# Decoder layer on one core: the scan's state and retrieval as 32 x 32 blocks, and the second quantile's edge counts on TensorE

## The reference

```
def step(S, inp):                       # per batch element and head, S is 16 x 16
    q_t, k_t, v_t, beta_t = inp
    retrieval = einsum('bhij,bhj->bhi', S, k_t)
    S = S + einsum('bhi,bhj->bhij', beta_t * (v_t - retrieval), k_t)
    o_t = einsum('bhij,bhj->bhi', S, q_t)
    return (S, o_t)
...
_, out_t = lax.scan(step, S0, (q, k, v, beta))          # 512 steps, 16 heads
...
attn = softmax(where(mask == 0, NEG, x @ ctx.T / 16)); x = attn @ ctx
...
s = 127 / quantile(abs(x), 0.995); q = clip(round(x * s), -128, 127) / s
out = quant(gelu(quant(h) @ ternary(w1).T)) @ ternary(w2).T
```

## Time and profile before

| | |
|---|---|
| median of 3 runs | 969.68 us |
| the profiled execution, its own time | 975.51 us |
| its span, first to last instruction | 973.6 us |
| mean granted TensorE clock, share of full | 0.95 |
| scan, first to last state matmul | 45.3 to 602.8 us |
| second quantile, first sample to scale | 888.8 to 923.5 us |

### The profile page before, as it was taken

How to read it: one execution, slowest core, us unless ns; L and a number is a source line. 1 busy time by engine, 2 the same in 40 slices (tenths; PEclk the granted TensorE clock), 3 DMA queues, 4 the chain that set the end, 5 groups by cost and what they waited for, 6 DMA issues and landing times.

```text
span 973.6 us, 19722 instructions
## 1 busy us (share of the span) xinstructions
PE 861.1 (88%) x6257; PEld 657.5 (68%) x6257; DVE 822.7 (85%) x2508; ACT 699.3 (72%) x1819; POOL 523.5 (54%) x501
## 2 busy tenths in 40 slices
PE   7899999999999999999999999879999813995285
PEld 6687887787787787787787777556666513443264
DVE  4789999989999999999999988756777787899797
ACT  4688888887788788788778766536777750895095
POOL 5446656665465565565455544445888860980100
PEclk9899999999999999999999999989999965998599
DMA  9900000000000000004000000133110000000023
GB/s 162 159 1 13 7 7 13 6 7 12 7 8 11 8 7 11 8 7 140 8 8 10 9 6 8 36 132 130 66 66 0 2 1 0 1 1 1 0 68 106
DMA packets 28573, 30.50 MB, mean 31 GB/s; under 512 B 5548, under 2 KB 23864, under 8 KB 28472
## 3 DMA queue, kind: packets, MB, share of 16 engines
q1 hardware_dynamic: 28256, 29.12, 11.9%
q10 hardware_dynamic: 216, 0.14, 0.1%
HBM read 20.85 MB, written 4.19 MB: 26 GB/s over the span
## 4 chain that ended last, share of the span: by engine, by line
PE 65%; ACT 15%; DVE 12%; issue 6%; POOL 1%; DMA 1%; ACTq 0%; POOLq 0%; DVEq 0%
PE ps L2002 10%; PE ps L1933 5%; PE psY L1971 5%; PE psX L1971 4%; PE ps L2118 4%; PE psG L1956 4%; PE ps L1994 4%; ACT arena L733 3%; PE psG L1950 3%; PE ps L2060 3%; PE psX L2139 3%; PE psY L2139 2%; PE ps L2325 2%; PE psG L1951 2%; ACT arena L698 2%
## 5 line engine op out<-in xcount | busy, mean ns | idle before, releaser
L523 POOL TENSOR_SCALAR_AFFINE_SELECT arena<-arena 128x2048 f32<-128x2048 f32 x32 | 64.5, 2015 | 163.3 <-DVE arena L1308 163.3
L538 POOL TENSOR_TENSOR work<-work,half 128x16 f32<-128x16 f32 x32 | 94.9, 2966 | 2.7
L527 POOL TENSOR_SCALAR_AFFINE_SELECT arena<-arena 128x2048 f32<-128x2048 f32 x32 | 92.1, 2879 | 2.2
L698 ACT ACTIVATE arena<-ps,nparity 32x128 f32<-32x128 f32 x248 | 76.2, 353 | 18.8 <-PE ps L1933 17.3
L1994 PE MATMUL ps<-work 32*128 32x256 f32 x512 | 82.6, 402 | 3.0 <-ACT arena L733 2.9
L733 ACT ACTIVATE arena<-ps 128x512 f32<-128x512 f32 x128 | 69.3, 593 | 16.6 <-PE ps L1994 15.8
L1994 PEld LDWEIGHTS ps<-work 32*128 32x128 f32 x512 | 53.5, 184 | 37.3 <-issue 28.3
L1327 DVE TENSOR_REDUCE arena<-arena 128x64 f32<-128x256 f32 (+1 forms) x96 | 65.9, 687 | 3.3
L1971 PE MATMUL psY<-work,arena 128*128 128x96 f32 (+1 forms) x512 | 61.7, 280 | 3.1 <-ACT arena L698 2.0
L1971 PEld LDWEIGHTS psY<-work,arena 128*128 128x128 f32 x512 | 60.0, 196 | 6.5 <-issue 6.5
L537 POOL TENSOR_SCALAR work<-work 128x16 f32<-128x16 f32 x32 | 8.1, 254 | 102.1 <-ACT work L750 102.1
(11 more groups left out here) (362 smaller groups left out, 2498.1 us busy)
## 6 DMA issues: line engine op xcount, KB each, us to landing
arena<-in_mask_BxSxS_ik SPq DMA_DIRECT2D x8, 1024.0 KB, 6.7
xs<-arena SPq DMA_DIRECT2D x256, 16.0 KB, 1.8
arena<-in_ctx SPq DMA_DIRECT2D x8, 512.0 KB, 4.2
out<-xs SPq DMA_DIRECT2D x32, 128.0 KB, 1.7
arena<-in_x SPq DMA_DIRECT2D x8, 288.0 KB, 17.5
arena<-in_L_ffn_w SPq DMA_DIRECT2D x2, 1024.0 KB, 20.6
arena<-in_x SPq DMA_DIRECT2D x16, 96.0 KB, 6.6
arena<-in_L_attn_w_qkvb SPq DMA_DIRECT2D x2, 512.0 KB, 5.9
```

The lines of the kernel that those rows point to most:

```text
L523: G.affine_select(out=keys, in_=keys, compare_op=ALU.is_ge, fill=0.0, base=0, pattern=[[0, NH], [1, P]], channel_multiplier=-1).then_inc(h ...
L527: G.affine_select(out=pairs, in_=pairs, compare_op=ALU.is_ge, fill=0.0, base=0, pattern=[[0, NH], [-CT, B], [0, CT]], channel_multiplier=1 ...
L538: own(G.tensor_tensor(root, length, half, ALU.pow))
L698: last = A.activation(sexp[rows, heads, cols], psS[rows, :].rearrange("p (h n) -> p h n", n=32)[:, heads, HD * e:HD * e + HD], ACT.Copy, s ...
```

## The change

State and retrieval no longer multiply by block-diagonal 128 x 128 matrices but by the 32 x 32 blocks themselves, each on its own rows and columns of the array. `kexp` is gone: `kt` is used as it stands. `sexp` becomes `scopy`, 32 columns per head, written by ScalarE alone in four ACTIVATEs over all 128 partitions. VectorE's `state` is gone. `keys_turned` waits for the state matmuls (`s_mm`) and stands behind `scale_near`. One matmul with zeros clears the whole bank of `psS` ahead of the first state update. In the second quantile all four edges are marked by VectorE and summed on TensorE, and VectorE keeps all candidates by itself.

```diff
 # GpSimd
-            G.memset(kexp.rearrange("p b n -> p (b n)"), 0.0).then_inc(consts, 1)
-            G.memset(sexp.rearrange("p h n -> p (h n)"), 0.0).then_inc(consts, 1)
+            G.memset(zeros, 0.0).then_inc(consts, 1)
...
-            pool.wait_ge(block_found, 1)
-            rest = slice(KEPT_ON_DVE, 2 * FF)
-            G.tensor_scalar(cand2[:, rest], cand[:, rest], bounds[:, 1:2], None, ALU.is_lt).then_inc(rest_marked, 1)
-            pool.wait_ge(rest_marked, 1)
-            G.tensor_tensor(cand2[:, rest], cand2[:, rest], cand[:, rest], ALU.mult).then_inc(rest_kept, 1)
 # ScalarE, state
                 for heads in (slice(0, NH // 2), slice(NH // 2, NH)):
-                    for r in range(2, 4):
-                        rows = slice(32 * r, 32 * r + 32)
-                        for e in range(2):
-                            cols = slice(32 * r + HD * e, 32 * r + HD * e + HD)
-                            last = A.activation(sexp[rows, heads, cols],
-                                                psS[rows, :].rearrange("p (h n) -> p h n", n=32)[:, heads, HD * e:HD * e + HD],
-                                                ACT.Copy, scale=nparity[rows, e:e + 1])
-                    last.then_inc(sexp_act, 1)
+                    for e in range(2):
+                        cols = slice(HD * e, HD * e + HD)
+                        last = A.activation(scopy[:, heads, cols],
+                                            psS[:, :].rearrange("p (h n) -> p h n", n=2 * HD)[:, heads, cols],
+                                            ACT.Copy, scale=nparity[:, e:e + 1])
+                    last.then_inc(state_copied, 1)
...
-                if exists(j) and j < NCK - 1:
-                    keys_spread(j)
...
-            A.activation(block_marks[1], block_marks[1], ACT.Copy, accum_out=counts[:, 1:2]).then_inc(part[1], 1)
 # VectorE
             def keys_turned(m):
-                v.wait_ge(kexp_ready, m)
+                v.wait_ge(s_mm, m)
...
-                if exists(j + 1) and j + 1 < NCK - 1:
-                    keys_turned(j + 1)
                 if exists(j + 2):
                     keys_normed(j + 2)
                 if exists(j + 1):
                     scale_near(j + 1)
-                    state(j + 1)
+                    if j + 1 < NCK - 1:
+                        keys_turned(j + 1)
...
-                    for e in range(EDGES - 1):
+                    else:
                         V.tensor_scalar(block_marks[e], values, edge[:, e:e + 1], None, ALU.is_ge).then_inc(edge_marked, 1)
-                    V.tensor_scalar(last_marks, values, edge[:, EDGES - 1:EDGES], None, ALU.is_ge, ALU.add,
-                                    accum_out=counts[:, EDGES - 1:EDGES]).then_inc(part[k], 1)
...
-                own(V.scalar_tensor_tensor(cand2[:, 0:n_own], values[:, 0:n_own], bounds[:, 1:2], values[:, 0:n_own],
-                                           ALU.is_lt, ALU.mult))
+                own(V.scalar_tensor_tensor(cand2[:, 0:n_cand], values, bounds[:, 1:2], values, ALU.is_lt, ALU.mult))
 # TensorE, state
-                pe.wait_ge(kexp_ready, j + 1)
+                pe.wait_ge(kt_ready, j + 1)
+                if j == 0:
+                    pe.wait_ge(ut_ready, 1)
+                    M.matmul(psS[:, :], zeros[:, 0:P], zeros, start=True, stop=True)
                 for b in range(NH // 2):
                     if b % 4 == 0:
                         pe.wait_ge(ut_ready, 2 * j + 1 + b // 4)
-                    last = M.matmul(psS[:, b * 64:b * 64 + 64], kexp[:, b, :], utm[:, b * 64:b * 64 + 64],
-                                    start=j == 0 and b == 0, stop=True, skip_group_check=True)
+                    for r in range(4):
+                        rows = slice(32 * r, 32 * r + 32)
+                        last = M.matmul(psS[rows, b * 64:b * 64 + 64], kt[rows, b * 32:b * 32 + 32],
+                                        utm[rows, b * 64:b * 64 + 64], start=False, stop=True, skip_group_check=True)
 # TensorE, retrieval
-                        pe.wait_ge(sexp_dve, 2 * m - 1 + h // (NH // 2))
-                        pe.wait_ge(sexp_act, 2 * m - 1 + h // (NH // 2))
+                        pe.wait_ge(state_copied, 2 * m - 1 + h // (NH // 2))
                     a, b = 1 if h == 0 else 0, 2 if h == NH - 1 else 3
-                    last = M.matmul(into[:, h - 1 + a:h - 1 + b], sexp[:, h, :], rows[:, h, a:b],
-                                    start=False, stop=True, skip_group_check=True)
+                    for r in range(4):
+                        rows = slice(32 * r, 32 * r + 32)
+                        last = M.matmul(into[rows, h - 1 + a:h - 1 + b], scopy[rows, h, :], streams[rows, h, a:b],
+                                        start=False, stop=True, skip_group_check=True)
 # TensorE, second quantile
-                    for e in (0, 2):
+                    for e in range(EDGES):
                         pe.wait_ge(edge_marked, e + 1)
                         for c in range(2 * FF // P):
-                            last = M.matmul(psY[:, e // 2:e // 2 + 1], block_marks[e][:, c * P:(c + 1) * P], ones_b[:, 0:1],
+                            last = M.matmul(psY[:, e:e + 1], block_marks[e][:, c * P:(c + 1) * P], ones_b[:, 0:1],
```

More of the change, by code:

```diff
@@ L278, in decoder @@
         edge_marks = cand2.bitcast(mybir.dt.uint8)
-        block_marks = [cand2[:, 0:FF].bitcast(BF16), cand2[:, FF:2 * FF].bitcast(BF16), gq[2][:, 0:2 * FF]]
-        last_marks = gq[2][:, 2 * FF:3 * FF].bitcast(mybir.dt.uint8)
-        KEPT_ON_DVE = 20 * KEPT
-        edges_counted = (EDGES, EDGES - 1)
+        block_marks = [half[:, k * 2 * FF:(k + 1) * 2 * FF] for half in gq[1:3] for k in range(2)]
+        edges_counted = (EDGES, 1)
         marks = [edge_marks[:, 4096 + 256 * e:4352 + 256 * e] for e in range(3)]
@@ L717, in updates_turned @@
                 last.then_inc(ust_ready, 1)
-            def keys_spread(j):
-                act.wait_ge(kt_ready, j + 1)
-                act.wait_ge(s_mm, j)
-                for r in range(4):
-                    rows = slice(32 * r, 32 * r + 32)
-                    last = A.activation(kexp[rows, :, 32 * r:32 * r + 32],
-                                        kt[rows, :].rearrange("p (b n) -> p b n", n=32), ACT.Copy)
-                last.then_inc(kexp_ready, 1)
             def attention_out(j, r):
@@ L1404, in near_products @@
                 V.tensor_tensor(PR[:, 1792:1920], later_keys(m, 2)[:, :, 1], key[:, :, 0], ALU.mult).then_inc(prod2, 1)
-            def state(j):
-                v.wait_ge(s_mm, j)
-                v.wait_ge(ret_mm, j)
-                for heads in (slice(0, NH // 2), slice(NH // 2, NH)):
-                    for r in range(2):
-                        rows = slice(32 * r, 32 * r + 32)
-                        last = V.tensor_tensor(sexp[rows, heads, 32 * r:32 * r + 32],
-                                               psS[rows, :].rearrange("p (h n) -> p h n", n=32)[:, heads],
-                                               block16[rows, 32 * r:32 * r + 32].rearrange("p (a n) -> p a n", a=1).broadcast_to([32, NH // 2, 32]),
-                                               ALU.mult)
-                    last.then_inc(sexp_dve, 1)
             def keys_turned(m):
-                v.wait_ge(kexp_ready, m)
+                v.wait_ge(s_mm, m)
                 V.transpose(kt, kq[m % 4][:, 0:CW]).then_inc(kt_ready, 1)
@@ L1963, in retrieval @@
                 first = 2 * (m % 4)
-                rows = padded[:, first:first + 3, :].rearrange("p z (k h t) -> p h z k t", k=2, t=CT)
+                streams = padded[:, first:first + 3, :].rearrange("p z (k h t) -> p h z k t", k=2, t=CT)
                 into = psR[m % 2][:, :].rearrange("p (h k t) -> p h k t", k=2, t=CT)
```

39 lines of the change are left out of this document (15 added, 24 removed).

## The result

The changed kernel takes **931.54 us** (median of 4 runs, 928.45 to 935.85) against 969.62 for the kernel before in the same comparison. The ratio is 0.9613, with a 95% interval of 0.9573 to 0.9652: 3.9% faster. The forecast was 940, range 910 to 985. The profiled execution took 935.85 (span 934.0), 39.7 less than that of before; the other runs were 4 to 7 us faster.

What follows compares the result with a forecast made beforehand. TensorE's work from retrieval to next state and VectorE's solve were both taken as bounds. 975.5 - 43 (scan) - 0.7 (quantile) + 0.9 (zero matmul) + 14 (clock) = 946.7, less 5.8 for the median: 940 us, range 910 to 985.

Steps and rivals of the forecast that it cites:

- the forecast's own case: Blocks in the scan's state and retrieval run together: 940 us, own range 910 to 962, chance 66%.
- State: State update on TensorE: 64 block passes in 16 rounds take 1.13 us instead of 1.89, -0.8 a chunk.
- Retrieval: Retrieval on TensorE: 128 block passes in 32 rounds take 2.9 us instead of 3.76, -0.9 a chunk.
- Both rivals of the blocks: State and retrieval: rounds no faster than 0.11 us (12%, 970 to 985), or blocks not running together (12%, near 1230).
- the serial case: Blocks of different rows don't run together in state and retrieval: +8.3 us a chunk, near 1230, chance 12%.
- Changes of shape: TensorE switching between whole-array and block passes, two block sections a chunk: net +0.5 us a chunk.
- Copying the state: State copied by ScalarE alone, VectorE's four copies gone: only a small TensorE wait goes, -0.2 us a chunk.
- The sum: All terms of a scan chunk: -0.8 - 0.9 + 0.5 - 0.2 = -1.4 us, so 16.9 a chunk.
- VectorE's limit of 16.2: Shortest scan chunk that VectorE's own work allows, 16.2 us, so at most 2.1 gained a chunk.
- The moved key transpose: VectorE's key transpose, now behind the state matmuls, finds the state done; the products behind it come 1.3 us earlier.
- The second quantile: Last edge marked instead of counted, VectorE keeping GpSimd's elements too: together -0.7 us, once.
- The clock: Blocks fill a quarter of the array and hold TensorE's clock up less well: 8 falls in the scan, +14 us.

Runs made afterwards that it cites:

- run of the state alone: The kernel before with only the state's update by 32x32 blocks, spread keys gone and key transpose moved, state still spread by VectorE and ScalarE: 969.0 us, ratio 0.9976.
- run of the second quantile alone: The kernel before with only the second quantile's part, all four edges marked by VectorE, which keeps all columns: 980.5 us in one run, the stage 13.77 us.
- All three edits together: The changed kernel with GpSimd's additions later, ternary factors in the solve ahead, context loads issued apart: 922.5 us, or 922.1 us with those loads placed later.

## Why the prediction was right, and where its steps were not

The outcome is the forecast's own case, and the two prices that carry it hold. State: -0.8 forecast, -0.80 measured. Retrieval: -0.9 forecast, -1.02 measured; that a round costs its columns and nothing for its weight loads is what the earlier trace rows had let expect. Both rivals of the blocks are out: a round is not 0.11, and the serial case exists, but here only where neighbours use the same block of the array.

*Changes of shape*, +0.5, was too much. In TensorE's order the next group begins 1.02 behind the start of the state where it was 1.73, and 2.67 behind that of the retrieval where it was 3.59: -0.71 and -0.92 of the -0.80 and -1.02, to which 0.13 comes ahead of the state and behind the key sums. That makes some +0.3. TensorE's work is down from 18.28 to 16.67, by 1.6.

*Copying the state*, -0.2, was the step with the wrong structure, though the prediction said in the same step that VectorE would be the new bound without that cut. The run of the state alone shows it: -0.8 without the copy's removal is worth 0.03, and with most of it removed 0.5. Terms of different engines had been added along one path, where the path changes engine within the chunk and each engine was within 0.4 us of it. The sum came out because the change takes from both.

*The sum*, -1.4 against -1.28: TensorE gave 1.6, and 0.32 went to the fold held beside GpSimd's additions. No step had this. That the sum is so near is partly luck: the 0.2 that it lacked on TensorE and the 0.32 that it left out stand against each other. VectorE's limit of 16.2 was right (16.1), but only where GpSimd leaves it alone; as changed it needs 16.98 and closes the loop. The kernel before had let it be seen once: its fold in the last chunk took 0.70 beside such an addition, and the prediction had read only its 0.29. The Trainium skill names the mechanism, in SBUF — State Buffer (SBUF: two separate sides): VectorE and GpSimd share one pair of ports, and an instruction of one of them that needs it, such as one of VectorE with two inputs in SBUF while GpSimd reads there, waits until the other's has ended. The rows on GpSimd's additions and masks agree: the fold's 0.84 and 0.70, the factors' 2.24 and, in the last chunk, a fold of 2.81 all end within about 0.15 us of GpSimd's instruction, while products that read PSUM keep their length. Another instruction of GpSimd does not: its root of the key norms (line 534, 2.93 us) reads SBUF too, and 38 of VectorE's instructions of line 1280 and 29 of line 1294, with both inputs in SBUF, lie wholly inside it and keep their 0.29 and 0.42. So which of GpSimd's instructions hold VectorE has to be read from the trace.

*The moved key transpose* waits for nothing, as said. The products come 2.1 earlier, not 1.3: the last of them ends 5.06 behind the transposes' start where it was 7.12. The 1.3 fits 1.72 of the copies less 0.43 for the key transpose, but that transpose stood ahead of the products before as well. *The zero matmul* takes 1.02 for its two passes, right ahead of the first update (42.72 to 43.74); the scan starts at the same time as before (first pair of transposes at 41.62, before 41.51), and its first chunk shows no loss (18.19 against 23.67). *The second quantile*, -0.7, measured -0.86.

*The clock*, +14, is the term that failed. In the profiled scan the clock stood at 1.2 GHz for 17.0 us (239.4 to 249.6, 430.5 to 437.3) against 6.8 before (49.5 to 53.0, 558.1 to 561.5); half of the difference, the prediction's own price, is 5. All irregular chunks together, falls, gaps and the start, cost some 11 us and had cost about as much before, so the net is about +1. The fall that the prediction read in the earlier trace rows had something else ahead of it, too:

```profile
555.91 1.61 PE L1994 MATMUL ps<-work 32*128 32x256 f32 x8 [0.84 <-ACT arena L733]
```

TensorE idled 0.84 us in that very stretch. In the run of the second quantile alone the same blocks stood behind a gap of 0.79 and the clock stayed up. The reason given, that blocks on a quarter of the array hold the clock up badly, does not hold for rounds of four or of two; it does for blocks one at a time, which this kernel has nowhere. The changed kernel's two falls in the scan came behind gaps of 2 us; what decides whether a gap brings one is open. The 13 us of the +14 that did not come, less 5 because 31 x 1.4 was really 38, is most of what lies between the 946.7 forecast for the profiled execution and 935.85.

The rule of the Trainium skill that was weighed (TensorE: Matmul & The Clock Gate, Part 1), no two matmuls less than about 25 ns apart, doesn't hold here: 64 passes of the state in 1.09 are 17 ns apart on average, and the retrieval's mostly 96-column passes 21. (Worked out against 1.89 and 3.76, that rule's 1.6 and 3.2 would have been 0.85 a chunk before the changes of shape, not the 0.7 given.) Nor does the Trainium skill's bank rule (TensorEngine Tiling (Array Packing), Restrictions and Gotchas): blocks of four different rows wrote one PSUM bank at once, on different partitions, in 2.74 us; serial, at 0.0825 each, they would take 10.6.

## What to carry to other kernels

When two engines are nearly level, follow the chain from engine to engine and price a change by the longest loop that is left after it, not as a sum along one engine: here -0.8 on TensorE alone was worth nothing, and with VectorE's copy gone 0.5. When an engine's work moves earlier, look at what then runs beside it; VectorE's instructions with both inputs in SBUF, and a TENSOR_SCALAR like that of the factors, should not meet GpSimd's additions or masks, and moving two of GpSimd's additions by 5 us is worth 6 us here. Small blocks make the program longer and use it up faster, so large loads are best issued away from them. All three edits together run in 922 us, 9 below the change and 5.3% below the kernel before.

## What the runs showed of the hardware that was not expected

- Passes on blocks of different rows and columns start some 17 to 21 ns apart on average and run at once, into one PSUM bank; on the same block of the array they run one after another, 0.0825 us for 96 fp32 columns.
- A series of single 32x32 blocks brings TensorE's clock from 2.4 to 1.2 GHz although it is busy without a gap, in all 31 retrievals of one profile; pairs (one profile) and fours of such blocks don't while TensorE has no gap.
- Retrievals of 256 TensorE instructions in 2.7 us can have gaps in which TensorE waits for nothing that the profile shows: of about 0.8 us with no load under way, of 2.0 to 2.2 beside loads of 1 to 3 MB. They end 2.3 to 2.75 us behind the start of a 16 KB packet on the instruction queue, so they are probably waits for instructions. The kernel before, with 51 packets on the instruction queue instead of 86, had no such gap in its retrievals.
- GpSimd's additions and masks hold VectorE's instructions with both inputs in SBUF until they end (0.29 becomes 0.70 to 2.81); its root of the key norms, 2.93 us long, holds none of them (0.29 stays 0.29).
